# An audio tower in one program: the steady bodies' fills and small operations set to other steps, and the values computed one body later

## The reference

```
# 1. frames: five neighbours, one linear layer, relu, batch norm over all tokens
y = relu(einsum('blf,of->blo', patches, W) + b)
h = (y - mean) * rsqrt(var + 1e-5) * gamma + beta
# 2. attention, 8 heads of 16
n = layernorm(h)
q, k, v = n @ Wq.T + bq, n @ Wk.T + bk, n @ Wv.T + bv      # split into heads
h = h + softmax(q @ k.T / 4) @ v  merged  @ Wo.T + bo
# 3. mixture of eight experts, one chosen for each token
n = layernorm(h)
gate, e = top_1(n @ Wr + br);  gate = softmax over the one chosen value
h = h + gate * (relu(n @ W1[e] + b1[e]) @ W2[e] + b2[e])
```

## Time and profile before

| | before |
|---|---|
| median of three executions | 1305.16 us |
| lowest, highest | 1304.66, 1306.34 us |
| profiled execution, its own time | 1302.61 us |
| its span, first to last instruction | 1300.8 us |
| mean granted TensorE clock | 0.963 of 2.4 GHz |
| PE busy | 1188.3 us, 91% |
| DVE busy | 1074.7 us, 83% |
| ACT busy | 954.8 us, 73% |
| POOL busy | 677.8 us, 52% |

### The profile page before, as it was taken

How to read it: one execution, slowest core, us unless ns; L and a number is a source line. 1 busy time by engine, 2 the same in 40 slices (tenths; PEclk the granted TensorE clock), 3 DMA queues, 4 the chain that set the end, 5 groups by cost and what they waited for, 6 DMA issues and landing times.

```text
span 1300.8 us, 53970 instructions
## 1 busy us (share of the span) xinstructions
PE 1188.3 (91%) x21394; PEld 735.8 (57%) x21394; DVE 1074.7 (83%) x2738; ACT 954.8 (73%) x2482; POOL 677.8 (52%) x895
## 2 busy tenths in 40 slices
PE   6479999999999999999999999999999845999996
PEld 3334545555554555454545555464544325999996
DVE  8478898989898999999898989999999634677774
ACT  5426878788787878787878878787877733677774
POOL 1162436556564847465655657483713334555654
PEclk9777999999999999999999999999999967999998
DMA  7145051432415050515143341504050323333331
GB/s 185 48 74 97 31 82 57 79 86 56 109 33 121 15 122 15 121 36 101 61 76 84 58 116 27 121 15 121 16 121 14 120 68 114 97 98 103 104 102 48
DMA packets 79582, 102.42 MB, mean 79 GB/s; under 512 B 15964, under 2 KB 73171, under 8 KB 78910
## 3 DMA queue, kind: packets, MB, share of 16 engines
q1 hardware_dynamic: 70192, 78.62, 26.4%
q0 software_dynamic: 8416, 20.22, 5.9%
q10 hardware_dynamic: 762, 0.55, 0.1%
HBM read 60.90 MB, written 39.00 MB: 77 GB/s over the span
## 4 chain that ended last, share of the span: by engine, by line
PE 68%; DVE 20%; issue 4%; POOL 1%; ACT 1%; DMA 1%; SPq 0%; POOLq 0%; another core or an unknown queue 0%; ACTq 0%; DVEq 0%
PE psum L1160 36%; PE psum L1225 14%; DVE half_max L1021 14%; PE psum L1296 7%; PE psum L1306 7%; PE psum L1165 2%; DVE rows L956 1%; PE psum L1287 1%; DVE merged_t L937 1%; ACT arena L773 1%; DVE by_tok L916 1%; DVE stats L882 1%; PE psum L1180 1%; DVE arena L928 1%; DMA arena<-max_rows 0%
## 5 line engine op out<-in xcount | busy, mean ns | idle before, releaser
L1021 DVE TENSOR_REDUCE half_max<-psum 128x1 f32<-128x373 f32 x1536 | 761.4, 533 | 87.5 <-PE psum L1160 77.9
L773 ACT ACTIVATE arena<-psum 128x373 f32<-128x373 f32 (+1 forms) x1536 | 652.6, 489 | 155.5 <-PE psum L1160 147.0
L1160 PE MATMUL psum<-k_rows,arena 96*32 96x373 bf16 x6144 | 525.7, 330 | 28.3 <-DVE half_max L1021 15.1
L1160 PE MATMUL psum<-arena,k_rows 98*32 98x373 bf16 x6144 | 516.0, 324 | 11.4 <-ACT arena L773 6.8
L1160 PEld LDWEIGHTS psum<-k_rows,arena 96*32 96x32 bf16 x6144 | 179.9, 95 | 260.3 <-DVE half_max L1021 172.5
L1225 PE MATMUL psum<-arena,values 128*32 128x373 f32 (+1 forms) x3072 | 314.6, 478 | 4.6 <-ACT arena L773 2.5
L1160 PEld LDWEIGHTS psum<-arena,k_rows 98*32 98x32 bf16 x6144 | 179.6, 96 | 125.5 <-ACT arena L773 51.3
L596 POOL DMA_INDIRECT routed_rows_dram<-rows,pos_i x96 | 98.1, 1021 | 165.9 <-PE psum L1160 112.6
L685 POOL DMA_INDIRECT out_dram<-arena,slot_id x102 | 116.5, 1143 | 93.6 <-DVE arena L1125 52.4
L1225 PEld LDWEIGHTS psum<-arena,values 128*32 128x32 f32 (+1 forms) x3072 | 98.4, 111 | 33.8 <-issue 6.7
L828 ACT COPY arena<-psum 128x128 f32<-128x128 f32 x102 | 27.1, 265 | 75.4 <-PE psum L1287 50.0
(11 more groups left out here) (192 smaller groups left out, 1443.1 us busy)
## 6 DMA issues: line engine op xcount, KB each, us to landing
arena<-q_parts_dram SPq DMA_DIRECT2D x192, 93.2 KB
k_rows<-k_parts_dram SPq DMA_DIRECT2D x192, 93.2 KB
arena<-routed_rows_dram SPq DMA_DIRECT2D x102, 130.0 KB
q_parts_dram<-q_part SPq DMA_DIRECT2D x48, 186.5 KB
k_parts_dram<-k_part SPq DMA_DIRECT2D x48, 186.5 KB, 1.9
arena<-in_x_t_dram SPq DMA_DIRECT2D x3, 703.1 KB, 18.1
seq<-in_w_dram SPq DMA_DIRECT2D x1, 2048.0 KB, 8.6
seq<-in_w_dram SPq DMA_DIRECT2D x8, 256.0 KB, 7.6
```

The costliest lines, as they stand in the source:

```text
L773: nc.scalar.activation(probs[0:kn(kt), G % N_P, j, :], st_bank[s % N_ST][0:kn(kt), 0:HALF], ACT.Exp).then_inc(s_exp, 1)
L1021: nc.vector.tensor_reduce(half_max[:, m:m + 1], mx_bank[m % N_MX][:, 0:HALF], AX.X, ALU.max)\
L1160: last = nc.tensor.matmul(dst[n:n + m], weights[:, n:n + m], moving, start=start, stop=stop)
```

## The change

The tables of the steady bodies get other numbers. The fills HTOK move from steps 1 and 4 to 9 and 13, V from 69 and 72 to 17 and 21, PROJ from 30 and 35 to 45 and 53, XNT from 47 and 50 to 49 and 57, Q and K by seven steps, MAX0 by one, RANK by two. V is now computed in the body ahead of the one that uses it (`STAGE` 1 in place of 2). VectorE's small operations are moved as well, and the residual gets a table (`REST_AT`, steps 48 and 55). ScalarE reads the steps of its readouts from `FILL_AT`; its gate exponential goes from step 75 to 86. No instruction's size changes, and in the steady bodies no instruction is added or removed.

```
-    LN1_AT = (22, 23, 24, 26, 27, 28)
-    LN2_AT = (42, 43, 44, 46, 47, 48)
-    T_AT, INV_AT, MULT_AT, BACK_AT = (54, 57, 5, 8), (60, 11), (62, 13), (16, 19)
-    ROUTE_AT = (59, 60, 61, 62, 63, 64)
+    LN1_AT = (17, 18, 19, 21, 22, 23)
+    LN2_AT = (57, 58, 59, 61, 62, 63)
+    T_AT, INV_AT, MULT_AT, BACK_AT, REST_AT = (65, 69, 9, 13), (73, 24), (74, 27), (40, 46), (48, 55)
+    ROUTE_AT = (75, 76, 77, 78, 79, 80)
...
-        STAGE = {"V": 2, "MAX1": 0, "HTOK": 2, "XNT": 2, "PROJ": -1, "Q": 2, "MAX0": 1, "K": 2, "RANK": -1}
+        STAGE = {"V": 1, "MAX1": 0, "HTOK": 2, "XNT": 2, "PROJ": -1, "Q": 2, "MAX0": 1, "K": 2, "RANK": -1}
+
+        FILL_AT = {(name, part): at for name, part, at in FILLS}
...
-                nc.scalar.copy(values[(i + 2) % 3][:, 3 * k:3 * (k + 1), :, 0:DH],
+                nc.scalar.copy(values[(i + 1) % 3][:, 3 * k:3 * (k + 1), :, 0:DH],
...
-                    if s == 75 and live(i, -1):
+                    if s == 86 and live(i, -1):
...
-                    if s in (32, 38) and live(i, -1):
-                        residual(i, i - 1, s // 38)
+                    if s in REST_AT and live(i, -1):
+                        residual(i, i - 1, REST_AT.index(s))
```

More of the change, by code:

```diff
@@ L283, in audio_tower @@
         FIRST_LOOP = 1
-        FILLS = (("HTOK", 0, 1), ("HTOK", 1, 4), ("PROJ", 0, 30), ("PROJ", 1, 35), ("MAX1", 0, 42), ("XNT", 0, 47),
-                 ("XNT", 1, 50), ("Q", 0, 54), ("Q", 1, 58), ("K", 0, 62), ("K", 1, 66), ("V", 0, 69), ("V", 1, 72),
-                 ("RANK", 0, 80), ("MAX0", 0, 88))
-        STAGE = {"V": 2, "MAX1": 0, "HTOK": 2, "XNT": 2, "PROJ": -1, "Q": 2, "MAX0": 1, "K": 2, "RANK": -1}
+        FILLS = (("HTOK", 0, 9), ("HTOK", 1, 13), ("V", 0, 17), ("V", 1, 21), ("MAX1", 0, 42), ("PROJ", 0, 45),
+                 ("XNT", 0, 49), ("PROJ", 1, 53), ("XNT", 1, 57), ("Q", 0, 61), ("Q", 1, 65), ("K", 0, 69), ("K", 1, 73),
+                 ("RANK", 0, 82), ("MAX0", 0, 89))
+        STAGE = {"V": 1, "MAX1": 0, "HTOK": 2, "XNT": 2, "PROJ": -1, "Q": 2, "MAX0": 1, "K": 2, "RANK": -1}
+        FILL_AT = {(name, part): at for name, part, at in FILLS}
         def live(i, ahead):
@@ L783, in body @@
                               .then_inc(s_o, 1)
[L785 removed]
+                    if s == FILL_AT["MAX1", 0] and live(i, 0):
                         max_out(i, i, 1, "MAX1")
[L787 to L798 removed]
+                    for part in range(2):
+                        if s == FILL_AT["HTOK", part] and live(i, 2):
+                            wait(act, s_ln_p, ln_p_done(i + 2))
+                            copy_out(i, "HTOK", part, h_cur[:, 3 * part:3 * (part + 1), :].rearrange("p t d -> p (t d)"))
+                        if s == FILL_AT["XNT", part] and live(i, 2):
+                            copy_out(i, "XNT", part, xn_t[:, 3 * D * part:3 * D * (part + 1)])
+                        for name in ("Q", "K"):
+                            if s - FILL_AT[name, part] in (0, 1) and live(i, 2):
+                                q_or_k(i, name, part, s - FILL_AT[name, part])
+                        if s == FILL_AT["V", part] and live(i, 1):
+                            values_out(i, part)
+                    if s == FILL_AT["MAX0", 0] and live(i, 1):
                         max_out(i, i + 1, 0, "MAX0")
[L800 to L802 removed]
+                    if s == 86 and live(i, -1):
                         act.wait_ge(s_gated, 3 * (i - 1) + 1)
```

17 lines of the change are left out of this document (1 added, 16 removed).

## The result

The change makes the kernel slower. Its runs took 1367.28, 1371.63, 1373.33 and 1385.41 us, median 1372.48, against 1304.91 of the kernel before on the same chip: 1.053 times as long, with an interval of 1.046 to 1.060. I had forecast 1292.7 and a range of 1276 to 1318.

A forecast was written before the change was run, and what follows sets the result against it. PE and DVE taking turns were taken to bound the body. Terms of -2.4 + 1.0 + 0.1 + 0.1 + 0.2 gave -1.0 us a steady body, -12.5 together: 1290.1 profiled, 1292.7 median, range 1276 to 1318.

The forecast's parts named there:

- The count by groups: Steady body, each four steps priced by the longer of PE and DVE: 58.7 falls to 56.3 us, -2.4.
- XNT, +1.0: Step 49: fill waits for VectorE to read PROJ of step 45; +1.0 us a body, bounds 0.8 and 1.3.
- RANK, +0.1: Step 82: fill waits for the router operation of step 80; +0.1 us a body, bounds 0 and 0.36.
- the rule: VectorE operations with two SBUF operands beside GpSimd's norms: the later blocked throughout; the trace showed 0.13 us more.
- Rival 2: GpSimd blocks VectorE products and router operations in groups 24, 72, 76: up to +1.6 us a body, around 1304; chance 0.12.
- MAX0, +0.1: MAX0 one step later, so its transfer to `q_rows` starts 0.32 later: +0.1 us a body, bounds 0 and 0.32.
- the heads' loads, hidden: K parts reach DRAM some 2 us later; heads read back are used only from step 36 on: no cost.
- The first sum: Body without scatters: count by groups -2.4, plus XNT 1.0, RANK 0.1 and MAX0 0.1, giving -1.2 us.
- The scatters, +0.2: Scatters back to back in steps 9 to 21: 1.45 us a body against 1.24 before, bounds 0.6 and 4.2.
- Rival 1: Scatters paid in full, 4.2 us in place of 1.24, steps 0 to 27 over 20: 1326, or 1312; chance 0.22.
- my four accounts: The forecast itself (chance 0.52), Rival 1 (0.22), Rival 2 (0.12), and a third rival, more is won, 1276 us (0.14).

The follow-up runs named there:

- the kernel with the three late pieces back: Changed kernel with HTOK fills at steps 1 and 4, residuals at 46 and 54, last ranks at 93 to 95: 1348.0 us, 1.033 (stalling).
- the values alone: Kernel before with only the V fills moved, to steps 9 and 16 from 69 and 72, `STAGE` 1: 1258.2 us, 0.987 (clear).
- the last kernel: The values alone, plus second V fill at step 20 and second norm's statistics at 44 to 50: 1260.7 us, 0.987 (clear).

## Why the prediction was wrong

The clear chips hold the scatters' cost at nothing and so test the rest of the sum; the stalling ones add the scatters.

**The count by groups, -2.4 a body.** It holds in kind and is a good half too generous: some 1.5 is what it was worth. Steps 0 to 27 were to fall from 17.6 to 16.9; on a clear chip they went from 17.63 to 17.42. For steps 28 to 95 the cleanest sight is the kernel with the three late pieces back: 40.5 on clear chips against 41.42, 0.9 less, where 1.7 less RANK and MAX0 were expected, 1.5; with the 0.44 that RANK cost (below) the count itself is worth 1.3 there. Nor does it hold group by group where its sum does. For the kernel before it gives 2.78 us for steps 16 to 19 and 2.20 for 20 to 23 (1.91 and the 0.87 and 0.29 of the prediction); a clear chip shows 2.27 and 2.73, and only the two together agree (the groups are measured at ScalarE's exponentials, so that VectorE's work can show one group later). So the agreement with body 1 to 0.3 us did not show that single groups were priced rightly. For one small move the count was right to 0.1 us (the values alone); in the second move of the last kernel it named the wrong work.

**XNT, +1.0.** Right: 0.89, released by `rows` of the residual, as forecast. The experiment that moves only the residual gives it back.

**RANK, +0.1.** Right in kind, short in size: in body 8 PE sits idle 0.28 us before the RANK fill until the router operation `onehot` (L986) is done, and steps 80 to 83 went from 2.17 to 2.61, 0.44, a little past the bound of 0.36.

**The ranks beside the split.** This term is missing, and it is the first step that failed. On a clear chip steps 88 to 95 grew by 1.9 us; moving three rank operations took 1.5 of them away. I had looked for blocked VectorE operations beside GpSimd's norms, because the last statistics stand there, and had moved the split in my text without asking which VectorE operations it would now lie beside. And I had dismissed the rule on the strength of a row that I misread: L975 beside the norm L386 lost 0.13 us, and I took that for the absence of a block. It is a short block. In body 8 of the changed kernel L909, which reads two operands from SBUF as well, begins 0.07 us into a tile of the norm, L388 (645.03 to 645.82), and takes 0.41 in place of 0.18 (DVE):

```profile
645.10 0.41 DVE L909 TENSOR_TENSOR max_parts<-neg_max,max_parts 128x24 bf16<-128x24 f32 x1
```

It ends 0.32 before the tile does, and so does every L909 of some 0.4 us; L975 ends 0.29 before its tile's end in all twelve steady bodies of the kernel before, after 0.32 to 0.34 us. So an operation that begins early in a norm tile waits until some 0.3 us into it (an estimate: 0.48, where L909 ends, less its own 0.18), and one that begins later doesn't wait: the products L928, which start 0.34 to 0.41 us into a tile, took 547 to 550 ns, as with GpSimd idle. The norm is a TENSOR_SCALAR with one full-sized input. The operations of the split of type TENSOR_TENSOR have two, and there the wait lasts nearly to the end: L1005 takes 0.20 us with GpSimd idle or late in the one-input L399, and 1.46 beside L401. L995, one of whose inputs stands in PSUM, took 0.20 inside that same two-input operation in body 8 of the kernel before (637.42, in 636.26 to 637.76). The Trainium skill, "SBUF — State Buffer", section "Who interferes with whom", says that a VectorE instruction with two inputs in SBUF contends with a GpSimd instruction that reads SBUF, by an exclusive lock. This trace agrees for GpSimd's two-input operations, to 0.06 us at the end; for its one-input ones it shows the wait for the first 0.3 of a tile's 0.79 us only. Rival 2 so named the right mechanism at the wrong place, and its price, 0.8 to 1.6 a body, covers what was measured. (Its times come out of its own terms as 1302 to 1312, not 1300 to 1310.)

**MAX0, +0.1; the heads' loads, hidden.** Nothing in the traces speaks against either; no run took them apart.

**The first sum.** Without scatters I had -1.2 a body (-2.4 + 1.2), where a clear chip shows +1.41. Of the 2.6 between, 1.5 is the rank block, 0.3 RANK, XNT gives 0.1 back, and the remaining 0.9 is the generous count.

**The scatters, +0.2.** The second step that failed, and the dearest. I took 1.45 in place of 1.24 a body, with bounds of 0.6 and 4.2. Held against a clear chip the change pays 5.0 (22.45 - 17.42), outside both. Two things went wrong. I assumed that each scatter costs a fixed lateness, 4.2 in all, of which no more than about the third that had reached the body before would reach it again; but late and close together they cost about 3.8 us of lateness at one place, of which three banks hide almost nothing. The seven bodies with a full clock lose 4.4, already past my upper bound. And I had no term for the clock: after such a stall PE is granted 0.50 in some bodies, in steps where its work is the bound, some 0.6 a body on the mean. What makes the stall stays open. Rival 1 was nearest of my four accounts. Its test (steps 0 to 27 over 20 us) came true with 22.45, and even at its highest price, 1326, it was 46 short: 0.8 x 12 = 10 of that for the deeper stall and the clock (5.0 in place of 4.2), 2.6 x 12 = 31 for what the first sum had wrong, and half of the remaining 5 because the profiled run, from which the bodies are read, lies 5.2 below its kernel's median (2.6 before). Rival 1 had the scatters right in kind and nothing of the rank block.

**Whether it was to be seen.** The slower sign was: the rank block alone, at the 1.5 that the later traces show, turns -1.0 into +0.5 a body. The operands of L395 and L399 (kernel before) stand in the code, and the trace of the kernel before has the block once, ahead of the first full body, where a product falls beside the split (DVE, POOL):

```profile
142.34 0.94 DVE L928 TENSOR_TENSOR arena<-by_tok,r_den 128x384 f32<-128x384 f32 x1
...
141.25 1.61 POOL L395 TENSOR_TENSOR q_rest<-q_full,q_part 128x746 f32<-128x746 f32 x1 [8.10 <-ACT q_part L744]
```

It takes 0.94 in place of 0.55. The size of the loss wasn't, since what the same scatters cost depends on where the kernel runs, from nothing to 5 us a body. The 1.24 that body 8 had over body 1 was the only sign of it, and the right answer to it was a wider range upward.

## What to carry to other kernels

When a table moves a long operation of GpSimd, list what now lies beside it on VectorE, and look at the number of SBUF inputs of both: a short two-input VectorE operation beside a long two-input GpSimd operation takes what is left of the long one's time. Hold such a row against where the other engine's operation ends, not against its length alone. When two like stretches of one trace differ only by one thing, as bodies 1 and 8 by the scatters, take its worst price as the range's end at least; here even that, 4.2, was short of 5.0. Scatters 2 us and more apart cost 1.24 us a body on a stalling chip and those 1.28 us apart 5.0, but the fills beside them had changed too, and spread scatters with the new fills were never run there: that spreading them helps is not shown. Move one thing at a time where a part alone can be had: on clear chips one of the parts was worth 1.3% and the whole cost 1.4%.

## What the runs showed of the hardware

- The same program is 2.1% slower in the first two comparisons (1303 to 1305 us) than on four other chips (1275 to 1278), and nearly the whole difference sits where GpSimd issues indirect transfers: body 1 is 17.66 us on both, body 8's first 28 steps 18.90 and 17.67.
- On the stalling kind, behind scatters 1.28 us apart TensorE starts three to five matmuls each 0.7 us for 3 us (body 8 of the change), while VectorE and ScalarE wait for it. The profile calls these gaps "issue". Neither instruction fetches nor longer transfers go with it: the change has one to three fetches under way in steps 4 to 11 of nearly every body on either kind, and the packets of the indirect queue take 0.20 us on the mean in steps 0 to 27 on both (0.202 and 0.195). The mechanism stays open.
- A TensorE busy 2.32 of 4.07 us in one group of four steps ran at the granted clock 0.50 in the next, which took 3.58 us in place of 2.30.
- A VectorE operation with two inputs in SBUF is held back by a two-input operation of GpSimd nearly to its end (1.46 us in place of 0.20), by a norm tile of 0.79 us only for its first 0.3 us (0.41 in place of 0.18).
